# Pairs of expert tiles share the turn and the row-half products of the last 64 inner columns; results and row transfers go in pairs

## The reference, cut to what matters

```python
w0 = ragged_dot(sorted_inputs, gate_proj, group_sizes)    # [tokens*8, 512] x [512, 192]
w1 = ragged_dot(sorted_inputs, up_proj, group_sizes)
inter = silu(w0) * w1                                     # 192 inner columns
expert_out = ragged_dot(inter, down_proj, group_sizes)    # x [192, 512]
output = einsum('BKE,BK->BE', per_token, routing_weights)
```

## Time and profile before

| | |
|---|---|
| median of 3 runs | 1563.96 us (1561.53 to 1567.16) |
| profiled execution, its span | 1567.3 us |
| expert stage in it | from about 940 us to the end |
| PE busy, whole span | 1435.0 us (92%) |
| DVE busy | 1153.4 us (74%) |
| ACT busy | 918.4 us (59%) |
| POOL busy | 1062.3 us (68%) |

### The profile page before, as it was taken

The page is one execution under the profiler, slowest core; times in us unless marked ns, Lnnn a source line. Parts: engine busy times, 40 slices in busy tenths (PEclk is TensorE's granted clock), DMA queues, the critical chain, the costliest instruction groups (busy, mean ns, idle before and its releaser), DMA issues. The chain is left out here.

```text
span 1567.3 us, 26498 instructions
## 1 busy us (share of the span) xinstructions
PE 1435.0 (92%) x6453; PEld 1073.9 (69%) x6454; DVE 1153.4 (74%) x2069; ACT 918.4 (59%) x1420; POOL 1062.3 (68%) x654
## 2 busy tenths in 40 slices
PE   6999878999999999999975559989999999999997
PEld 3444556666666666666644238878988888898886
DVE  5888897888888878888878786656666666565554
ACT  6777677666667666766646664444544444444442
POOL 2222287999999989999941235757666676666675
PEclk9999989999999999999988759999999999999999
DMA  8232557888899889988869416889998899888876
GB/s 314 96 111 98 180 132 144 179 197 205 192 196 217 186 195 178 221 188 195 176 150 336 159 31 159 193 193 209 198 200 192 191 206 201 203 186 190 189 146 118
DMA packets 106416, 283.95 MB, mean 181 GB/s; under 512 B 16641, under 2 KB 18850, under 8 KB 95090
## 3 DMA queue, kind: packets, MB, share of 16 engines
q0 software_dynamic: 43520, 155.57, 50.0%
q1 hardware_dynamic: 60322, 123.12, 26.4%
q10 hardware_dynamic: 2512, 4.52, 0.8%
HBM read 152.28 MB, written 135.08 MB: 183 GB/s over the span
## 5 line engine op out<-in xcount | busy, mean ns | idle before, releaser
L1156 POOL TENSOR_TENSOR B_E<-B_dtu,B_BC 128x512 f32<-128x512 f32 (+3 forms) x121 | 309.3, 2670 | 16.7 <-DMA B_BC<-bc_d 16.7
L2080 POOL DMA_INDIRECT out_x<-D_y,D_rows x144 | 243.8, 1693 | 75.4 <-issue 43.6
L889 ACT ACTIVATE bank<-B_dtv,negA 128x512 f32<-128x512 f32 x256 | 173.5, 690 | 159.8 <-DVE B_E L1024 98.1
L1024 DVE TENSOR_TENSOR_SCAN B_E<-bank,B_E 128x512 f32<-128x512 f32 x192 | 230.2, 1214 | 42.5 <-ACT bank L889 34.8
L1162 POOL TENSOR_TENSOR B_E<-B_E,B_BC 128x1536 f32<-128x1536 f32 x64 | 234.0, 3656 | 34.5 <-DVE B_E L1024 29.8
L2045 POOL DMA_INDIRECT D_rows<-rows_d,D_source x144 | 155.9, 1083 | 129.0 <-DMA out_x<-D_y,D_rows 62.3
L806 PE MATMUL bank<-B_Wd,B_inter 128*128 128x512 f32 x512 | 231.9, 606 | 9.0 <-DVE X L1011 5.3
L1906 ACT ACTIVATE D_xT_hi<-bank 128x512 fp32r<-128x512 f32 x147 | 88.1, 599 | 231.5 <-PE bank L1815 167.8
L1826 PE MATMUL bank<-W_gu_hi,D_xT_hi 128*128 x584 | 202.4, 347 | 14.5 <-ACT D_xT_hi L1906 13.9
L1968 DVE TENSOR_TENSOR D_xT_lo<-bank,D_xT_hi 128x512 fp32r<-128x512 f32 x147 | 101.3, 689 | 141.1 <-ACT D_xT_hi L1906 108.7
L1827 PE MATMUL bank<-W_gu_lo,D_xT_hi 128*128 x584 | 199.2, 341 | 0.0
(11 more groups left out here) (327 smaller groups left out, 3263.7 us busy)
## 6 DMA issues: line engine op xcount, KB each, us to landing
y_d<-B_E POOLq DMA_DIRECT2D x64, 1024.0 KB, 10.7
B_BC<-bc_d SPq DMA_DIRECT2D x128, 256.0 KB, 6.2
W_raw_gu<-in_wgu SPq DMA_DIRECT2D x64, 384.0 KB
W_raw_d<-in_wd SPq DMA_DIRECT2D x64, 256.0 KB
X<-in_x SPq DMA_DIRECT2D x4, 1024.0 KB, 9.2
y_d<-A_du SPq DMA_DIRECT2D x4, 1024.0 KB, 4.0
dt_d<-A_dtv SPq DMA_DIRECT2D x4, 1024.0 KB, 3.9
dtu_d<-A_dtu SPq DMA_DIRECT2D x4, 1024.0 KB, 4.1
```

Of the source, the lines that this page charges most:

```text
L889: act.activation(dA[m % 2][:, :], dtv[:, c, :], ACT.Exp, scale=negA[:, c, n:n + 1]).then_inc(dA_done, 1)
L1024: v.tensor_tensor_scan(state, dA[m % 2][:, :], E[:, s % NR, c, :], 0.0, ALU.mult, ALU.add).then_inc(s_done, 1)
L1156: g.tensor_tensor(E[:, s % NR, c:end, :], dtu[:, at:at + end - c, :], spread(BC[op % NBC][:, :], end - c), ALU.mult).then_inc(dbu_done, 1)
L2080: g.indirect_dma_start(a["out"], bass.IndirectOffsetOnAxis(ap=rows[i][:, ROW - 1:ROW].bitcast(U32), axis=0), ysb[:, i, :], None, compute_o ...
```

## The change

The engines work on pairs, an even tile and the odd one behind it.

- **Inner columns.** `inner` keeps only the first 128. The last 64 of the even and of the odd tile go side by side into `rest`, and are turned once for a pair, so that the even tile's lie in partitions 0 to 63 and the odd tile's in 64 to 127.
- **Down products.** Three full ones for each tile (`down`), and after those of the odd tile six with 64 rows for the pair (`down_rest`): the upper half of the array works for the even tile and the lower for the odd one, into the two banks. The even result is thus complete only behind the odd tile's products.
- **Odd tile's weights.** VectorE copies the lower half of the second part of the down weights into `odd_w` (two copies for each pair), so that a pair may span two experts.
- **Results.** ScalarE copies the even tile's result in the odd iteration and behind the weight splits; VectorE copies the odd one's. TensorE waits for the even copy before the next pair's first down product.
- **GpSimd.** In an even iteration both gathers of the pair are issued, for t+6 and t+7, ahead of the scatter of t; in an odd one only the scatter.
- **Weights.** ScalarE's high part of the down weights is one activation with 1024 columns in place of two with 512; the two `clear` memsets go.

```diff
+            def down(i, buf):
+                hi, lo = (w[:, ds(buf, 1), 0:D].rearrange("p o n -> p (o n)") for w in (W.d_hi, W.d_lo))
+                first = slice(0, P)
+                pe.matmul(py[i % 2][:, :], iT_hi[i % 2][:, first], hi, start=True, stop=False)
+                pe.matmul(py[i % 2][:, :], iT_lo[i % 2][:, first], hi, start=False, stop=False)
+                pe.matmul(py[i % 2][:, :], iT_hi[i % 2][:, first], lo, start=False, stop=False)
+
+            def down_rest(buf):
+                low, high = slice(0, MR), slice(MR, P)
+                for n, (x, w, h) in enumerate(((iT_hi, W.d_hi, 0), (iT_lo, W.d_hi, 0), (iT_hi, W.d_lo, 1))):
+                    even = pe.matmul(py[0][:, :], x[1][low, P:2 * P], w[low, ds(buf, 1), D:2 * D].rearrange("p o n -> p (o n)"),
+                                     start=False, stop=n == 2, tile_position=(0, 0))
+                    odd = pe.matmul(py[1][:, :], x[1][high, P:2 * P], odd_w[high, h, :], start=False, stop=n == 2, tile_position=(MR, 0))
+                even.then_inc(y_ps, 1)
+                odd.then_inc(y_ps, 1)
...
+                        if i % 2 == 0:
+                            pe.wait_ge(y_sb, q * HALF + (i // 2 + 1))
+                            even = buf
+                        down(i, buf)
+                        if i % 2:
+                            pe.wait_ge(odd_done, q * HALF + (i // 2 + 1))
+                            down_rest(even)
...
-                        act.wait_ge(y_ps, t + 1)
-                        act.activation(ysb[:, i, :], py[i % 2][:, :], ACT.Copy).then_inc(y_sb, 1)
...
+                        if i % 2:
+                            result(t - 1, i - 1)
...
+                        if i % 2 == 0:
+                            odd = v.snap(code[i] & (CODE_SHARE - 1), min_val=0, max_val=NE - 1)
+                            v.wait_ge(W.d_split, odd + 1)
+                            buf = ring(v, odd, 0, NSLOT)
+                            for h, w in enumerate((W.d_hi, W.d_lo)):
+                                copy = v.tensor_copy(odd_w[MR:P, h, :], w[MR:P, ds(buf, 1), D:2 * D].rearrange("p o n -> p (o n)"))
+                            copy.then_inc(odd_done, 1)
+                        else:
+                            v.wait_ge(y_ps, t + 1)
+                            v.tensor_copy(ysb[:, ds((q & 1) * HALF + i, 1), :].rearrange("p o n -> p (o n)"), py[1][:, :]).then_inc(y_odd, 1)
...
-                        done = 32 * q + 16 * (i // 4 + 1)
-
-                        g.wait_ge(added[(i + 2) % 4], done + (16 if i % 4 >= 2 else 0))
-                        g.sem_inc(passed)
-                        gather((i + AHEAD) % UNROLL)
+                        if i % 2 == 0:
+                            for j in (i, i + 1):
+                                g.wait_ge(added[(j + 2) % 4], landed(q, j) + (16 if j % 4 >= 2 else 0))
+                                g.sem_inc(passed)
+                                gather((j + AHEAD) % UNROLL)
+                        done = landed(q, i)
...
-                        g.wait_ge(y_sb, t + 1)
+                        g.wait_ge((y_sb, y_odd)[i % 2], q * HALF + (i // 2 + 2 - i % 2))
```

More of the change, by code:

```diff
@@ L1707, in __init__ @@
         self.d_hi, self.d_lo = (sb(f"d_{h}", [P, NSLOT, 2 * D], F32R) for h in ("hi", "lo"))
[L1708 to L1712 removed]
+        self.ld, self.gu_hi_done, self.d_hi_done, self.gu_split, self.d_split = (sem(n) for n in ("ld", "gu_hi_done", "d_hi_done", "gu_split", "d_split"))
     def split_down_hi(self, act, raw, i):
[L1716 to L1718 removed]
+        return act.activation(self.slot(self.d_hi, i), self.slot(self.raw_d, raw), ACT.Copy)
     @staticmethod
@@ L1744, in block_d @@
         xT_hi, xT_lo = ([sb(f"xT_{h}{i}", [P, KC * P], F32R) for i in range(2)] for h in ("hi", "lo"))
-        sil, inner = [sb(f"sil{i}", [P, M]) for i in range(2)], [sb(f"inner{i}", [P, 2 * P]) for i in range(2)]
-        iT_hi, iT_lo = ([sb(f"iT_{h}{i}", [P, 2 * P], F32R) for i in range(2)] for h in ("hi", "lo"))
+        sil, inner = [sb(f"sil{i}", [P, M]) for i in range(2)], [sb(f"inner{i}", [P, P]) for i in range(2)]
+        rest, odd_w = [sb(f"rest{i}", [P, 2 * MR]) for i in range(2)], sb("odd_w", [P, 2, D], F32R)
+        iT_hi, iT_lo = ([sb(f"iT_{h}{i}", [P, (1 + i) * P], F32R) for i in range(2)] for h in ("hi", "lo"))
         ysb = sb("y", [P, UNROLL, D])
@@ L1835, in turn_inner @@
             def turn_inner(i):
-                for c in range(2):
-                    mm = pe.transpose(piT[i % 2][:, c * P:(c + 1) * P], inner[i % 2][:, c * P:(c + 1) * P], ident[:, :])
+                mm = pe.transpose(piT[i % 2][:, 0:P], inner[i % 2][:, :], ident[:, :])
+                if i % 2:
+                    mm = pe.transpose(piT[1][:, P:2 * P], rest[i // 2 % 2][:, :], ident[:, :])
                 mm.then_inc(iT_ps, 1)
+            def down(i, buf):
[12 more added lines that the diff above has]
+                odd.then_inc(y_ps, 1)
             pe.wait_ge(tokens_done, 1)
@@ L1920, in split_down, with result @@
                 W.split_down_hi(act, raw, buf).then_inc(W.d_hi_done, 1)
+            def result(n, i):
+                act.wait_ge(y_ps, n + 2)
+                act.activation(ysb[:, i, :], py[0][:, :], ACT.Copy).then_inc(y_sb, 1)
+            act.sem_inc(y_sb)
             turn(0, 0)
@@ L1957, in weigh @@
                 weight = rows_all[:, ds(share, 1)]
-                def twice(t):
-                    return t.rearrange("p (o n) -> p o n", o=1).broadcast_to([P, 2, MR])
-                v.scalar_tensor_tensor(out=inner[i % 2][:, 0:P], in0=sil[i % 2][:, 0:P], scalar=weight,
+                side = i % 2 * MR
+                v.scalar_tensor_tensor(out=inner[i % 2][:, :], in0=sil[i % 2][:, 0:P], scalar=weight,
                                        in1=pgu[i % 2][:, M:M + P], op0=ALU.mult, op1=ALU.mult)
-                v.scalar_tensor_tensor(out=inner[i % 2][:, P:2 * P].rearrange("p (o n) -> p o n", o=2), in0=twice(sil[i % 2][:, P:M]), scalar=weight,
-                                       in1=twice(pgu[i % 2][:, M + P:2 * M]), op0=ALU.mult, op1=ALU.mult).then_inc(inner_done, 1)
+                v.scalar_tensor_tensor(out=rest[i // 2 % 2][:, side:side + MR], in0=sil[i % 2][:, P:M], scalar=weight,
+                                       in1=pgu[i % 2][:, M + P:2 * M], op0=ALU.mult, op1=ALU.mult).then_inc(inner_done, 1)
             def turn_lo(tile, i):
@@ L2046, in gather, with landed @@
                                      bass.IndirectOffsetOnAxis(ap=source[i // HALF][:, i % HALF:i % HALF + 1].bitcast(U32), axis=0)).then_inc(ld_rows[i], 16)
+            def landed(q, i):
+                return 32 * q + 16 * (i // 4 + 1)
             for i in range(AHEAD):
```

10 lines of the change are left out of this document (5 added, 5 removed).

## The result

| | before | after |
|---|---|---|
| median of the runs | 1562.74 us | 1685.63 us (1683.47 to 1689.87) |
| ratio | | 1.0787, 95% interval 1.0758 to 1.0816 |
| span of the profiled execution | 1567.3 us | 1681.7 us |

What follows compares the result with a forecast made beforehand. POOL's closed chain was to bound the kernel: L 6.15 + 3.37 = 9.52 us a pair; 958.3 + 71 x 9.52 + 1.99 + 9.2 = 1645.4 us span, less 3.3, so 1642 us, range 1590 to 1690.

Steps and rivals of the forecast that it cites:

- The mechanism: POOL, expert stage: two scatters, a landing and the second gather form one closed chain of 9.52 us a pair.
- L: POOL: time from a scatter's start to the gather that needs its landing; taken as 6.15 us, ends 5.53 and 6.77.
- The signs: Expected after: about 42 scatters in 200 us, some 4 us POOL idle before gathers, PE over 80 us on turned rows.
- the first gather inside the odd scatter's L: POOL: the pair's first gather, released 1.99 us earlier, was to have its 1.38 us within the odd scatter's landing time.
- One reason given for a short L: POOL: no gather stands between the second scatter and its landing, which may make the landing time shorter.
- The upper end, 6.77: POOL: median scatter-to-gather distance in us, taken as the landing time's upper end; gives 10.14 us a pair, 1686 us.
- -0.34 us a pair: PE: saving if half-row products run side by side, nine products' time against ten, less a turn; 7.82 us a pair.
- PE sets the pace: Kernel before, expert stage: PE, busy 99.01 of 100 us, was named the bound, at 8.16 us a pair.
- rival 1: Expert stage: PE stays the bound and the change saves 24 us, giving 1540 us; 6% chance.
- rival 3: TensorE's clock falls in the new gaps: 11.7 us a pair, 1797 us; 4% chance.
- The 43 us of the prediction: POOL: up to 72 x 0.6 us longer if DVE's new copies disturb scatters; left out of the sum.
- ACT, drains, memsets: ACT misses absorbed by PE's 1.7 us slack a pair; memsets nothing; drain waits nothing, up to 4 us an event.

Runs made afterwards that it cites:

- experiment 4: Weight transfers in the loop cut to a sixteenth of their columns: changed kernel 1661.20 us (1.0555 of before), kernel before 1547.26 us (0.9823).
- experiment 7: Changed kernel with one gather ahead of each scatter, its six half-row products replaced by six full ones: 1588.22 us, 1.0129 of the kernel before.
- experiment 1: Changed kernel with one gather ahead of each scatter, the rest of the change kept: 1579.05 us, 1.0063 of the kernel before.
- experiment 5: Kernel before, three of five down products: 1560.14 us; also five tiles ahead 1568.33; also small weight transfers, six ahead 1527.41; all products, five ahead 1566.73.
- experiment 3: Changed kernel with its paired gathers, but five tiles ahead instead of six: 1585.84 us, 1.0116 of the kernel before.
- experiment 6: Kernel before with two of an expert's four weight transfers in flight at a time: 1585.39 us, 1.0079 of the kernel before.

## Why the prediction was right, point by point

- **The mechanism** was right: a closed chain on POOL of two scatters, a landing and the second gather. Its terms, forecast and measured (means of 71 pairs): two scatters 1.99 and 2.05 us; L 6.15 and 6.56; gather and issue 1.38 and 1.40; cycle 9.52 and 10.01. First scatter 958.3 and 960.0 us. 71 x 0.49 + 1.7 = 36.5 us is the whole distance from the forecast span of 1645.4 to 1681.7. The signs came, with one in another place: 40 scatters in 200 us (42 forecast), 3.7 us of idle time a pair on POOL before gathers (some 4), but PE's 80 us of waiting stand ahead of the turns, for the gathers, and only 2.5 us at the gate products, for turned rows.
- **Which landing ends the wait.** The prediction puts the first gather inside the odd scatter's L, as if the odd landing always came last. In 50 of 71 pairs it does. In the other 21 the even scatter landed late (6.82 us on average), and the second gather followed the first at once, with nothing left to wait for. The sum of the terms holds in both cases, since L is taken to the gather's start.
- **The term that was mis-sized is L.** I took the middle between the shortest distance and the median, on the ground that many distances were only upper bounds. One reason given for a short L, that no gather stands between the odd scatter and its landing, is wrong: the pair's first gather goes out there (1250.84 above, between 1247.21 and 1252.84). The gather behind the odd scatter starts 0.4 us later after it than the first gather after the even one (6.56 and 6.17; 0.3 in experiment 4). The upper end, 6.77, was nearer, and it is why the time lies at the upper edge of the range, 4 us inside. That 6.77 is near is in part luck: it is a median that contains gathers which waited for nothing.
- **PE.** Half-row products do run side by side: in the changed kernel the two of a step start at the same time, and the next two (1258.34) 0.23 us later.

```profile
1257.45 0.39 PE L1840 MATMUL bank<-W_d_lo,D_iT_hi 128*128 x1
...
1258.10 0.39 PE L1845 MATMUL bank<-W_d_hi,D_iT_lo 64*128 x1
1258.11 0.39 PE L1847 MATMUL bank<-D_odd_w,D_iT_lo 64*128 64x512 f32 x1
...
1258.34 0.39 PE L1847 MATMUL bank<-D_odd_w,D_iT_hi 64*128 64x512 f32 x1
```

  My -0.34 us a pair left the gaps out. Each costs PE some 0.2 us. On the way into the half-row products, from 1257.45 to 1258.10, it is 0.65 us where 2 x 0.23 would do; behind the even tile's down products, in experiment 7, L1840 starts at 1250.30, L1820 at 1250.65 and L1821 at 1250.92, 0.62 us where 0.23 + 0.18 would do. With three of them a pair I estimate that PE needs 0.6 - 0.34 = 0.3 us more, not less; experiment 1 shows 9 to 10 us in 72 pairs, 0.13 each. There was no saving even where POOL did not hide it. The Trainium skill's rule that changing the tiling mode drains TensorE (TensorEngine Tiling (Array Packing), Tiling Modes) is borne out by the way in; the trace puts 0.37 us of idle weight loading there (23.0 us in 63 times).
- **"PE sets the pace"** was half of the truth: weight transfers bound at least as much (experiments 4 and 5). The 8.16 us a pair came from a dense stretch; over all 71 pairs it is 8.46. And with POOL's chain out of the way the change gives 1579 us (experiment 1) and not rival 1's 1540. It did not matter for the sign, since POOL's chain is longer than both.
- **The clock** did fall at times: 0.93 and 0.94 in the windows above, against 1.00, with PE idle for rows before. Nothing of rival 3 shows in the time: POOL's terms, none of which is PE's, make up the whole cycle of 10.01 us.
- **DVE.** The two copies into `odd_w` take 0.45 and 0.46 us (0.5 assumed). They do disturb POOL, but little. The 91 scatters of the changed kernel that overlap neither a copy nor a weight subtraction on DVE last 1.60 us on average and 1.63 at most; the 20 that overlap only copies last 1.71, and up to 1.82; in experiment 1 it is 1.59 (59) and 1.71 (38). That is 0.1 us each, some 2 us in the changed kernel, and the mean of all scatters is 1697 ns against 1693. The Trainium skill's rule (GPSIMD Engine Reference, Specifications) names VectorE instructions with two SBUF inputs and those in a two-port mode. The first kind shows, as before; the copies have one input and cost what is said above, and no run shows whether they are of the second kind. The 43 us of the prediction, whose 0.6 us a pair has no row behind it, did not come.
- **ACT, drains, memsets** show nowhere: behind the first no scatter waits for a result, and the two scatters of a pair are over 2.2 us apart only in 8 of 72 pairs, each time because the even one itself took 2.19 us or more.

## What to carry to other kernels

When asynchronous steps are regrouped, write down for each wait which transfer it needs and how many instructions of that queue lie between: if a queue waits for the transfer that it issued last, its whole round trip stands in every round, whatever the busy shares say. Regrouping that keeps one issued transfer behind the one waited for cost about 0.5% here (experiment 3 against 1). And look at the chain that ended last before naming a bound: an engine that is 99% busy can have an equal beside it, and a saving on it is then worth little (experiment 5), as is one on the equal alone when a third chain is close behind (experiment 6).

## What the hardware showed that was not expected

- Of two 128-row accumulating scatters issued 1.9 us apart, the second releases the gather behind it 0.3 us later after its own start, with hardly any weight traffic (6.13 against 5.83 us). The pair's first gather goes out before the second scatter has landed, so the cause is open.
- Weight loading stands idle for about 0.4 us ahead of a product when only three 512-column products stand behind the last wait (127 times in 540 us), and hardly ever with five (19 times). In PE's work it costs 0.2 us.
- Going from whole-array to half-row products costs the same 0.4 us of weight loading, 0.2 us of PE.
- A copy of 64 x 512 from SBUF to SBUF on VectorE and a scatter that GpSimd issues at the same time lengthen each other in part: the scatter from 1.60 to 1.71 us on average, and a copy from the 0.42 us that it takes alone to 0.72 at the most.
